# New orders in setup, tail and feed-forward of an AdaLN block with windowed attention and a dense mixture of experts; the last three batches normalised by GpSimd

## What is computed

```
mod = (silu(c) @ wmod).reshape(8, 6, 1, 128)
sa, ca, ga, sb, cb, gb = ...
ga = (2 * (ga >= 0) - 1) * maximum(abs(ga), 0.25)
gb = (2 * (gb >= 0) - 1) * maximum(abs(gb), 0.25)
h = layernorm(x) * (1 + ca) + sa
x = x + ga * attn_block(h)
h = layernorm(x) * (1 + cb) + sb
x = x + gb * experts(h)

def attn_block(h):
    r = h
    n = layernorm(h, ln1)
    q, k, v = n @ wq, n @ wk, n @ wv
    ctx = windowed_attention(q, k, v, 64)
    r = ctx @ wproj + bproj + r
    n = layernorm(r, ln2)
    return gelu(n @ w1 + b1) @ w2 + b2 + r

def experts(x):
    w = routing_weights(x, Wr, temperature)
    return sum over e of w[e] * ((silu(x @ Wg[e]) * (x @ Wu[e])) @ Wd[e])
```

## Time and profile before

| what | value |
|---|---|
| median of 3 runs | 287.16 us (284.64 to 289.91) |
| profiled execution: time | 289.58 us |
| profiled execution: span from first to last instruction | 287.8 us |
| busy share of the span: PE, DVE, ACT, POOL | 81%, 77%, 48%, 26% |
| mean granted TensorE clock | 0.941 |

### The profile page before, as it was taken

One profiled execution on the slowest core, in us unless ns is written; L12 is line 12 of the kernel. 1 busy time (PEld: TensorE's weight loads), 2 busy tenths in 40 slices (PEclk: granted clock), 3 DMA queues, 4 the chain that ended last, 5 costly groups with the idle time before them and its releaser, 6 DMA issues.

```text
span 287.8 us, 10048 instructions
## 1 busy us (share of the span) xinstructions
PE 232.8 (81%) x4145; PEld 182.9 (64%) x4145; DVE 221.5 (77%) x614; ACT 138.3 (48%) x250; POOL 75.7 (26%) x106
## 2 busy tenths in 40 slices
PE   6768577577778797697795998499798999899991
PEld 4335345466667676576673676379586897788991
DVE  1687678889879866759647358987789986989795
ACT  2564313676668566354584437334732366123210
POOL 6432233253526312211210046064000350030300
PEclk9997957999999979989997799989999999999997
DMA  5418725544634563630053000000000001001011
GB/s 146 148 47 211 201 53 143 114 141 120 172 86 129 136 177 76 179 79 7 7 162 141 0 2 1 2 0 0 1 0 3 0 2 36 0 1 39 0 36 39
DMA packets 21172, 20.43 MB, mean 71 GB/s; under 512 B 2668, under 2 KB 18568, under 8 KB 21128
## 3 DMA queue, kind: packets, MB, share of 16 engines
q1 hardware_dynamic: 21128, 19.80, 25.6%
HBM read 11.13 MB, written 8.13 MB: 67 GB/s over the span
## 4 chain that ended last, share of the span: by engine, by line
PE 46%; DVE 19%; issue 10%; ACT 6%; SPq 4%; DMA 3%; POOL 3%; DVEq 0%; ACTq 0%; POOLq 0%
PE bank L659 7%; DVE nm L1105 5%; PE bank L444 4%; PE pair L641 4%; PE pair L402 4%; PE pair L643 3%; PE bank L618 3%; PE pair L642 3%; PE pair L418 3%; DVE xh L1046 3%; PE pair L495 3%; DVE acc L1422 2%; ACT prob L746 2%; DMA earl<-in_earlier 2%; PE bank L454 2%
## 5 line engine op out<-in xcount | busy, mean ns | idle before, releaser
L746 ACT ACTIVATE prob<-pair 128x1024 f32<-128x1024 f32 x32 | 32.8, 1026 | 28.3 <-PE pair L418 28.2
L1105 DVE TENSOR_REDUCE nm<-pair 128x16 f32<-128x1024 f32 x32 | 39.0, 1220 | 9.6 <-PE pair L402 9.4
L886 POOL TENSOR_TENSOR rs<-ve,mhalf 128x2 f32<-128x2 f32 (+1 forms) x24 | 21.1, 881 | 93.5 <-DVE ve L1043 93.5
L836 ACT ACTIVATE sg<-pair 128x512 f32<-128x512 f32 x32 | 18.9, 601 | 43.5 <-PE pair L643 42.0
L659 PEld LDWEIGHTS bank<-wds,hh 128*128 128x128 f32 x256 | 32.3, 191 | 7.0 <-issue 5.4
L659 PE MATMUL bank<-wds,hh 128*128 128x128 f32 x256 | 33.7, 277 | 2.7 <-DVE acc L1422 2.3
L1422 DVE SCALAR_TENSOR_TENSOR acc<-bank,rt,acc 128x128 f32<-128x128 f32 x112 | 32.7, 342 | 1.2 <-PE bank L659 0.2
L641 PE MATMUL pair<-h3rest,wpart 128*128 128x512 f32 x64 | 27.5, 430 | 2.0 <-ACT sg L836 2.0
L1324 DVE TENSOR_TENSOR hh<-sg,pair 128x512 f32<-128x512 f32 x32 | 21.8, 682 | 6.6 <-ACT sg L836 5.6
L444 PE MATMUL bank<-prob,vb 128*32 128x64 f32 x1024 | 22.6, 230 | 4.1 <-ACT prob L746 2.7
L643 PE MATMUL pair<-h3part,wpart 128*128 128x512 f32 x64 | 25.1, 393 | 0.0
(11 more groups left out here) (153 smaller groups left out, 471.8 us busy)
## 6 DMA issues: line engine op xcount, KB each, us to landing
stack_scratch<-parts SPq DMA_DIRECT2D x16, 216.0 KB, 2.5
qst<-stack_scratch SPq DMA_DIRECT2D x16, 216.0 KB, 3.6
kst<-stack_scratch SPq DMA_DIRECT2D x16, 216.0 KB, 4.1
stack_scratch<-parts SPq DMA_DIRECT2D x16, 144.0 KB, 2.4
stack_scratch<-parts SPq DMA_DIRECT2D x16, 72.0 KB, 2.6
out_x<-fin SPq DMA_DIRECT2D x4, 256.0 KB, 2.3
xs<-in_x SPq DMA_DIRECT2D x1, 768.0 KB, 5.8
qst<-mt SPq DMA_DIRECT2D x32, 8.0 KB
```

The costliest lines, as they stand in the source:

```text
L746: act.activation(prob[:, :, :, pair % 2, :], psb[:].rearrange("p a (h q) -> p a h q", h=H2), ACT.Exp).then_inc(exp_done, 1)
L1105: dve.tensor_reduce(groups, psa[:].rearrange("p a (h k) -> p a h k", h=H2), AX_X, ALU.max, negate=True).then_inc(max_done, 1)
```

## The change

1. `gate` becomes a function for either engine: sign (`is_ge`, less 0.5), times sign, `max(0.125) * 4`, times sign; four instructions in place of four. `gate(GA)` stays on DVE, behind the whole of step 7. `gate(GB)` leaves DVE and goes to POOL, behind `token_rest(3)` and in front of `finish(0)`.
2. For b = 5, 6, 7 POOL forms `xh` and `x1h`, two tensor_scalar each; the second normalising has statistics of its own (`st2`, `mv2`, `ve2`, `rs2`). DVE keeps only the statistics.
3. Setup: POOL's `cut_m(0, 0)` stands in front of `norm_x(3)`.
4. First step: DVE's list is written out anew (`first_step`), and PE's `scores_a(1, 1)` stands behind `scores_b(0, 1)`. PE's `turn_sums` waits explicitly for the `normalise` before it.
5. The late loads are two: `w1`, `w2` are issued one step earlier with a semaphore of their own; the experts' weights keep their place.
6. Step 7: DVE's `normed_tokens(2)` stands in front of `normalise(7, 0)`; POOL does `bias_residual(0)` at the end of step 7.
7. Feed-forward: POOL's `bias_residual(g)` for g = 1, 2, 3 stands in front of the power of `ln3`, and every `weight_rest` or `token_rest` waits until the `ln3_out` (or `normed_tokens`) going on is done. The pieces of the weights are cut in another order, so that PE waits for two of them at u = 0 and for all four at u = 4.

```diff
+        gsign = sb("gsign", [P, B, D])
...
+        def gate(eng, c, sign, step):
+            eng.wait_ge(mod_ready, after(mod_ready, 2 * B))
+            g_v = modb[:, :, c, :]
+            eng.tensor_scalar(sign, g_v, 0.0, 0.5, ALU.is_ge, ALU.subtract).then_inc(step, 1)
+            eng.wait_ge(step, after(step, 1))
+            eng.tensor_tensor(g_v, g_v, sign, ALU.mult).then_inc(step, 1)
+            eng.wait_ge(step, after(step, 2))
+            eng.tensor_scalar(g_v, g_v, 0.125, 4.0, ALU.max, ALU.mult).then_inc(step, 1)
+            eng.wait_ge(step, after(step, 3))
+            eng.tensor_tensor(g_v, g_v, sign, ALU.mult).then_inc(step, 1)
+            eng.wait_ge(step, after(step, 4))
...
-                if b == B - 2:
+                if b == B - 3:
                     load_late()
+                elif b == B - 2:
+                    load_moe()
...
             def turn_sums(b, eo):
                 pe.wait_ge(pvs_ready, after(pvs_ready, 2 * b + eo + 1))
+                pe.wait_ge(norm_step, after(norm_step, 3 * (2 * b + eo)))
...
-                if ahead:
+                if ahead and (b or eo):
                     scores_a(b + 1, 2 * eo + 1)
                 probs_v(b, 2 * eo)
                 scores_b(b, 2 * eo + 1)
+                if b == eo == 0:
+                    scores_a(1, 1)
...
-            pe.wait_ge(late_loaded, after(late_loaded, 128))
+            pe.wait_ge(late_loaded, after(late_loaded, 32))
             first(0, 0)
...
-            pe.wait_ge(wrest_ready, after(wrest_ready, PIECES))
             for u in range(E * NG):
+                if u in (0, E // 2):
+                    pe.wait_ge(wrest_ready, after(wrest_ready, PIECES // 2 if u == 0 else PIECES))
...
             def norm_x(b):
...
-                    pool.wait_ge(ln_dve, after(ln_dve, 14 * b + 7))
+                    pool.wait_ge(ln_pool, after(ln_pool, 5 * b + 1))
+                    for k in range(TPB):
+                        pool.tensor_scalar(xh[:, k, :], xs[:, TPB * b + k, :], mv[:, k, 0:1], rs[:, k:k + 1],
+                                           ALU.subtract, ALU.mult).then_inc(x_normed, 1)
...
             def second_root_x(b):
...
+                    root(rs2[:], ve2[:], TPB, ln_pool)
+                    pool.wait_ge(ln_pool, after(ln_pool, 5 * b + 5))
+                    pool.wait_ge(xt_done, after(xt_done, b))
+                    for k in range(TPB):
+                        pool.tensor_scalar(x1h[:, k, :], h1[:, k, :], mv2[:, k, 0:1], rs2[:, k:k + 1],
+                                           ALU.subtract, ALU.mult).then_inc(x1h_ready, 1)
...
             first_root_x(3)
+            cut_m(0, 0)
             norm_x(3)
-            cut_m(0, 0)
...
             root_tokens(NG - 1)
-            bias_residual(0)
+            pool.wait_ge(xh2_ready, after(xh2_ready, NG))
             weight_rest(0)
+            bias_residual(1)
             root_normed(0)
-            bias_residual(1)
+            normed(0)
             weight_rest(1)
-            weight_rest(2)
+            bias_residual(2)
             root_normed(1)
-            bias_residual(2)
+            normed(1)
+            weight_rest(2)
+            bias_residual(3)
+            root_normed(2)
+            normed(2)
+            token_rest(0)
             weight_rest(3)
-            token_rest(0)
-            root_normed(2)
-            bias_residual(3)
             token_rest(1)
             root_normed(3)
+            normed(3)
             token_rest(2)
             token_rest(3)
-            pool.wait_ge(gate_step, after(gate_step, 8))
+            gate(pool, GB, gsign[:], gate_b_step)
             with pool.Fori(0, NG - 1) as g:
                 finish(pool, g)
...
             def step(b):
...
-                    ln_d(b + 4)
...
+                else:
+                    normed_tokens(group)
                 normalise(b, 0)
...
-                    ln_b(b + 5)
...
             for g in range(NG - 2):
                 combine(g)
                 ln3_stats(g)
                 ln3_out(g)
-                if g == 0:
-                    gate(GB)
```

134 lines of the change are left out of this document (74 added, 60 removed).

## The result

| what | before | changed kernel |
|---|---|---|
| median | 287.13 us (4 runs, 284.64 to 289.91) | 294.64 us (4 runs, 292.60 to 296.10) |
| profiled execution: time, span | 289.58, 287.8 | 293.59, 291.7 |
| mean granted TensorE clock | 0.941 | 0.933 |

The ratio is 1.0286, 95% interval 1.018 to 1.040: the change costs 2.9%. Predicted was a gain of 5.2 us, inside 276 to 287.

The account below looks back on a forecast made before the run. No engine bounds the whole; each stretch has its own waits between engines. Terms -3.5 - 6.3 - 1.4 + 6.0 = -5.2 us take 289.6 to 284.4, or the median 287.2 to 282.0; range 276.0 to 287.0.

Parts of the forecast that it names:

- The second gate: On POOL between token_rest(3) and finish(0): gate of 8.0 us delays accumulate(1, 0) by 6.0 us; bounds 4 and 8.5.
- The slower rival: Second gate's two tensor_scalar on GpSimd take t each, not 1.3 us: time 282.0 + 2(t - 1.3); chance 0.08.
- Setup and attention: Setup and attention steps: -3.5 us from cut_m ahead of res, the first step and norms leaving DVE; bounds 0.5 to 6.9.
- the orders of setup and first step: Setup and first attention step: cut_m(0, 0) ahead of res worth 1.0 us, the first step's new order 0.3.
- The norms: Attention, two DVE pairs that waited for POOL's power at 59.91 and 66.57: worth 1.3 and 0.9 us; other four nothing.
- End of attention: Last attention step up to combine(0): 168.1 in place of 171.73, -3.6 us, through loads, xh and an earlier normalise(7, 1).
- Feed-forward and first units: From combine(0) into the experts: experts start 5.9 us earlier, End of attention included; -7.7 us in all after first units.
- the charge of 1.2 for the bias row: Feed-forward: bias_residual(g+1) on POOL beside DVE's combine(g) costs one POOL instruction, 1.2 us, making DVE's chain 7.2 per group.
- Gate hidden: Rival at the second gate: slack in PE and DVE behind 235 removes the +6.0, giving 276.0; chance 0.15.
- Attention nothing: Rival in attention: steps equally long with or without norms, only 0.5 of 3.5 us comes, giving 285.0; chance 0.22.
- Port contested: Rival in feed-forward: weight_rest and bias_residual on POOL cost each of three combine 1.3 us more, giving 285.9; chance 0.15.
- the signs of the forecast: Profile signs: combine(0) some 7 us earlier, PE idle about 4 before experts, POOL gate about 8, acc waiting about 6.

Follow-up runs that it names:

- the ladder: `gate_early` with eleven GpSimd instructions (copies, tensor_scalar, tensor_tensor of several lengths) behind its last `finish`, to price each; 1024 elements took 1.04 to 3.64 us.
- setup_old: `split_norms` with the setup and the first step in the order of before on all engines; ratio 0.9722 (0.964 to 0.980).
- split_norms: `split_wait` with the normalising of batches 5 to 7 back on VectorE; ratio 0.9527 (0.943 to 0.962).
- three pairs of kernels: Normalising of batches 5 to 7 on GpSimd against VectorE, otherwise alike: ratios 0.9869 and 0.9866, 0.9684 and 0.9697, 0.9556 and 0.9527.
- ga_late: `gate_early` with gate(GA) on VectorE behind normalise(7, 1) in place of ahead of it; ratio 0.9695 (0.964 to 0.975).
- before_gate: The kernel before with only gate(GB) moved to GpSimd behind token_rest(3), in the new form; ratio 1.024 (1.006 to 1.041).
- ff_old: `gate_early` with POOL's feed-forward rows, waits and weight pieces in the old order; ratio 0.9796 (0.973 to 0.986).
- bias_late: `gate_early` with bias_residual(g) waiting for the third instruction of combine(g-1) in place of the first; ratio 0.970 (0.961 to 0.979).
- gate_early: The changed kernel with gate(GB) on GpSimd issued behind token_rest(1), ahead of root_normed(3); ratio 0.9869 (0.974 to 0.999).
- gate_mid: The changed kernel with gate(GB) on GpSimd behind bias_residual(0), at the end of attention's last step; ratio 0.992 (0.988 to 0.997).
- split_wait: Changed kernel: gate(GA) behind normalise(7, 1), gate(GB) split between POOL and DVE, token_rest(0) ahead of root_normed(2), weight_rest(3) waiting for routing; ratio 0.9556, median 274.8 us.

## Why the prediction was wrong, step by step

**The second gate, "+6.0".** Right in the mechanism and the place, wrong in one term, and this is the largest part of the miss: 10.6 us in place of 6.0. The step that failed is "Two have one input: at most four copies of 256 ... I take 1.3". Each took 3.64 us. The two tensor_tensor, taken at 2.4, were 2.38 and 2.34. 2 x (3.64 - 1.3) = 4.7 brings the gate from 8.0 to 12.7, with its shorter waits 12.3, and DVE's wait from 6 to 10.9. The upper bound failed as well: "8.5 if the one-input instructions cost as much as the two-input ones" took it for granted that one input cannot cost more than two. The slower rival had the true form, 282.0 + 2(t - 1.3): with t = 3.64 it gives 286.7. So the right price alone would have turned the forecast gain into no change; the loss needed the next step's miss as well. I had given it 0.08 and the forecast 0.40, for want of a row; a copy was the wrong nearest row. The sentence on the Trainium skill (GPSIMD Engine Reference, "Engine selection") pointed the same wrong way, to 0.85 us; the ladder shows 1.04 for the copy, which comes near, and 2.79 to 3.64 for arithmetic, which does not.

**Setup and attention, "-3.5".** In the changed kernel's profile it was +0.5 at the last maxima, 4.0 us from the forecast, the second part of the miss. Of its parts, the orders of setup and first step, taken at 1.3, are worth 1.8 us in the stretch where they act, and by the ratios of `setup_old` and `split_norms` more, 2 to 9: the queue in front of `mp` was 2.0 us long, because the wait of the row in front counts with its 1.07. The norms, taken at 2.2 for the two pairs that waited for POOL's power, show no worth in three pairs of kernels, whose intervals reach to some 2 us. That step fell as far as the runs can tell. On POOL the pair takes 1.58 us in place of 0.60, and in the means the steps from the ninth to the twenty-first maxima give back what the first had won; that the one causes the other is not shown. My bound for the pair, "at most 1.27", was the gate's mistake again. Why this one profile shows none of the order's 1.8 is scatter as far as the runs tell: its stretches behind the ninth maxima are 0.5 and 1.5 us above the mean of their kind.

**End of attention, "-3.6".** Measured -3.4 from the last maxima to `combine(0)` (31.30 us before, 27.93 after). "What is late next is gate(GA)" was right: `ga_late` takes the 2.00 us wait away. "PE runs this stretch at the lower clock in either kernel" was wrong: the granted clock there was 0.59 before and 1.00 in the changed kernel. And one thing that went was not in the sum: the `xh` of the last tokens, 3.02 us before, takes 1.12. That the total fits is in part luck.

**Feed-forward and first units, "-5.9" and "-7.7 in all".** From `combine(0)` on that is a gain of 2.3 at the experts' start and 4.1 in all; measured 3.4 and 3.9. The numbers stood, and the reason was half wrong. (The working's own terms from `combine(2)` on add up to 191.4 and 192.7, where it writes 191.6 and 193.0.) `combine(1)` and `combine(2)` 7.39 and 7.44 us apart, PE's stop of 3.13 (predicted 4) for `token_rest(0)`, the first experts 23.7 us behind `combine(0)` (predicted 24.9) came as told, and the charge of 1.2 for the bias row was 0.95. But by the profiles of `before_gate` and `ff_old` the gate's leaving DVE is all of it that can be seen: the reorder wins 2.6 in two rounds and loses it in PE's stop and in the routing steps beside three POOL rows (1.28, 1.22 and 1.20 us in place of 0.2), which I did not count. The waits of 0.40 and 0.69 us, said to go, stayed as they were.

**The rivals.** Gate hidden: false at this place, true ahead of `root_normed(3)`. Attention nothing: what this profile shows, not what the ratios of `setup_old` and `split_norms` show. Port contested: the bias row does collide, but by the rows PE covers it, and the ratio of `bias_late` leaves that open. The gate's own length, "about 8 us", stood among the signs of the forecast and not among those that would prove it wrong; that was the number to watch.

**The sum.** With the measured terms +0.5 - 3.4 - 3.9 + 10.6 = +3.8 us, the spans' 3.9 but for rounding. Against the forecast's -5.2 the gate is 4.6 of the miss, setup and attention 4.0, the other two 0.4. The medians lie 7.5 apart; where the other 3.6 us arise no row shows.

## What to carry to other kernels

Before work moves to another engine, price each kind of instruction on that engine by a row of that very kind; with none, leave the upper bound open and let the rival that depends on it have its weight. Look next at where the moved work stands in its new queue: the same four instructions, 12.3 to 12.7 us, cost 10.6 between `token_rest(3)` and `finish(0)`, 1.4 in front of `root_normed(3)`, and nothing that shows when the one-input halves stood in POOL's idle time and the two-input halves in DVE's. And add up only what one edit gives alone: here, as far as the profiles tell, one removal carried all that a reorder seemed to gain.

## What the runs showed of the hardware that I had not expected

- GpSimd's arithmetic with one input is dearer than with two: at 128x1024 float32 a tensor_scalar of two operations 3.64 us, of one 2.79, a tensor_tensor 2.41, a copy 1.04. At 128 elements, in the same order, 0.64, 0.54, 0.45 and 0.29.
- In `gate_early` GpSimd's tensor_tensor held a two-input instruction of VectorE until it was over (2.88 us for 0.68), and its tensor_scalar of 3.64 us did not: beside it a two-input one took 0.68 and another 0.92, while the tensor_scalar itself grew to 3.95. The Trainium skill (SBUF, State Buffer page, "Who interferes with whom") has the first; by its rule a GpSimd instruction that reads SBUF would hold VectorE's in both cases, and the second measurement differs from it. VectorE's own tensor_scalar of 1024 elements beside GpSimd's took 1.41 us for 0.69 in `gate_mid`, with GpSimd's at 4.49, and 0.68 in `split_wait`; what decides between the two is not shown.
- PE stops in the midst of rows, at fixed instructions of its program, in every kernel (in front of the last 24 of a row of L449: 0.89 to 3.36 us), while nothing in the trace holds it. What sets the length stays open.
- The granted clock behind such a wait is not the same each time: `gather_context(7)` took 1.93 us at a granted clock of 0.53 behind a wait of 2.00 in `gate_early`, and 1.13 us at 1.00 behind the same wait in the changed kernel. In both PE had been busy at 1.00 right before that wait.
